# A four-stage graph network kernel: its last stage rewritten with full float32 matmuls, shared statistics and a later fourth norm

## The reference, cut to what matters

```python
x = _layernorm(x + _L0_gnn_ref(...))   # two graph convolutions and LSTMs
x = _layernorm(x + _L1_gnn_ref(...))   # masked attention
x = _layernorm(x + _L2_gnn_ref(...))   # aggregation, two layers with batch norm
x = _layernorm(x + _L3_gnn_ref(...))   # below, J = 128 here

adj_0, adj_1, adj_2 = diag(adj), triu(adj, 1), tril(adj, -1)
h = einsum('bjf,kfo->kbjo', x, W)      # W is [3, 128, 128]
out = sum over k of einsum('ij,bjo->bio', adj_k, h[k]) + bias
```

## Time and profile before

| | us |
|---|---|
| median of 3 runs (lowest, highest) | 1770.82 (1768.04, 1772.41) |
| the profiled execution | 1766.66 |
| its span, first to last instruction | 1764.9 |
| busy in the span: PE, DVE, ACT, POOL | 1515.1, 1347.8, 1071.9, 461.5 |
| mean granted TensorE clock | 0.951 of 2.4 GHz |

### The profile page before, as it was taken

How to read it: one execution, slowest core, us unless ns; L and a number is a source line. 1 busy time by engine, 2 the same in 40 slices (tenths; PEclk the granted TensorE clock), 3 DMA queues, 4 the chain that set the end, 5 groups by cost and what they waited for, 6 DMA issues and landing times. The chain is left out here.

```text
span 1764.9 us, 29113 instructions
## 1 busy us (share of the span) xinstructions
PE 1515.1 (86%) x9300; PEld 1252.2 (71%) x9300; DVE 1347.8 (76%) x3193; ACT 1071.9 (61%) x2018; POOL 461.5 (26%) x699
## 2 busy tenths in 40 slices
PE   3998999899899989966999999999995996777775
PEld 3888888788888888964767767777774554555554
DVE  3578777767776777776888888888884556888886
ACT  3675675566665756744666666666662664666665
POOL 2122212212211222123333333333332002334333
PEclk9999999999999999987999999999997997989888
DMA  2000000000000000000000000000000000111111
GB/s 91 1 1 25 13 1 13 25 1 13 13 13 12 1 25 13 1 14 1 19 19 12 18 18 12 18 18 12 18 18 24 0 0 24 60 59 63 56 59 48
DMA packets 19515, 37.58 MB, mean 21 GB/s; under 512 B 3312, under 2 KB 4848, under 8 KB 19312
## 3 DMA queue, kind: packets, MB, share of 16 engines
q1 hardware_dynamic: 18576, 34.49, 6.1%
q10 hardware_dynamic: 864, 2.11, 0.3%
HBM read 19.81 MB, written 16.78 MB: 21 GB/s over the span
## 5 line engine op out<-in xcount | busy, mean ns | idle before, releaser
L377 PE MATMUL banks<-early_rounded 128*128 128x128 f32 (+3 forms) x1424 | 457.3, 321 | 63.6 <-DVE early_rounded L968 31.3
L378 PE MATMUL banks<-early_rounded 128*128 128x128 f32 (+3 forms) x1424 | 452.8, 318 | 0.0
L379 PE MATMUL banks<-early_rounded 128*128 128x128 f32 (+3 forms) x1424 | 452.6, 318 | 0.0
L773 ACT ACTIVATE early_scratch<-banks,consts 128x256 f32<-128x256 f32 (+2 forms) x624 | 312.1, 566 | 129.5 <-PE banks L379 115.0
L377 PEld LDWEIGHTS banks<-early_rounded 128*128 128x128 f32 x1424 | 279.0, 196 | 88.8 <-issue 41.4
L378 PEld LDWEIGHTS banks<-early_rounded 128*128 128x128 f32 x1424 | 279.5, 196 | 14.3
L379 PEld LDWEIGHTS banks<-early_rounded 128*128 128x128 f32 x1424 | 279.0, 196 | 13.8
L644 POOL CAST early_rounded<-early_scratch 128x512 fp32r<-128x512 f32 (+2 forms) x160 | 94.0, 597 | 550.5 <-DVE early_scratch L963 550.5
L487 POOL TENSOR_TENSOR consts<-consts 128x4 f32<-128x4 f32 (+1 forms) x112 | 125.9, 1124 | 151.3 <-DVE consts L461 148.8
L377 PE MATMUL banks<-kept_rounded 128*128 128x128 f32 (+2 forms) x384 | 142.7, 372 | 21.9 <-DVE kept_rounded L1117 5.5
L727 ACT ACTIVATE attention_rounded<-banks 32x512 fp32r<-32x512 f32 (+1 forms) x160 | 94.5, 591 | 98.4 <-PE banks L1305 67.9
(11 more groups left out here) (168 smaller groups left out, 3213.6 us busy)
## 6 DMA issues: line engine op xcount, KB each, us to landing
early_scratch<-in_x_dram SPq DMA_DIRECT2D x16, 512.0 KB, 3.6
x_away<-attention_scratch SPq DMA_DIRECT2D x32, 256.0 KB, 2.0
late_scratch<-x_away SPq DMA_DIRECT2D x32, 256.0 KB, 2.7
out_dram<-late_scratch SPq DMA_DIRECT2D x32, 256.0 KB, 2.0
x_all<-in_WihT_dram ACTq DMA_DIRECT2D x1, 1024.0 KB, 5.5
x_all<-in_WhhT_dram ACTq DMA_DIRECT2D x1, 768.0 KB, 7.2
x_all<-in_Wqkv_dram ACTq DMA_DIRECT2D x1, 192.0 KB, 9.8
kept_scratch<-in_W_dram SPq DMA_DIRECT2D x1, 192.0 KB, 2.4
```

Source lines behind the costliest of these rows:

```text
L377: pe.matmul(out, wt[0], mv[0], start=start, stop=False)
L378: pe.matmul(out, wt[1], mv[0], start=False, stop=False)
L379: return pe.matmul(out, wt[0], mv[1], start=False, stop=stop)
L773: nc.scalar.activation(gate_f[lane][gate][:, 0:cols], bank(bank_set("lstm", n, unit), gate)[:, 0:cols], ACT.Tanh if gate == G else ACT.Sig ...
```

## The change

Everything lies in the last stage. The mixing is one full float32 matmul for each batch and the sums are three, with x3, the adjacency parts and the weights as they are; the high and low parts of all of these go, and with them ACT's and POOL's work on x3, DVE's subtraction of each mix, and the splitting of two late weights earlier in the program. DVE works in rounds (`late_round`): the fourth norm's add and sums for the group four behind, the third norm's add and sums for the newest, the third norm's application for the one behind it, and then one set of small operations over eight columns, four of each norm. POOL raises eight columns at once. ACT applies the fourth norm six groups behind the newest, first in its head. There are two buffers for y3, y4, the mixes and the shifts, and four for x3. The diff leaves out what the functions printed above show of the old code.

```diff
+    def late_groups(eng, order, do):
+        def head_of(head, at):
+            for what, part, late in order:
+                if not isinstance(head, int) or 0 <= head - late < GROUPS:
+                    do(what, part, head - late, (at - late) % 4)
+        warm = 8
+        for head in range(warm):
+            head_of(head, head)
+        with eng.Fori(warm // 4, GROUPS // 4) as i:
+            for at in range(4):
+                head_of(i * 4 + at, at)
+        for head in range(GROUPS, GROUPS + max(late for _, _, late in order)):
+            head_of(head, head)
...
-        splits2 = [("w1", w1_r), ("w3", w3_r), ("hatT", hatT_r), ("adjk", adjk_r)]
+        splits2 = [("w1", w1_r), ("hatT", hatT_r)]
...
-        r2 = Area(sb("late_rounded", 6 * GC, F32R))
-        mix_r = pair(r2, GB * 3 * P)
-        f3 = Area(sb("late_scratch", 14 * GC))
-        hid_f = [[f3.take(GC) for _ in range(2)] for _ in range(2)]
-        z_f = f3.take(GC)
-        y3 = f3.take(GC)
-        x3_f = [f3.take(GC) for _ in range(2)]
-        y4 = f3.take(GC)
-        oT_f = f3.take(GC)
+        f3 = Area(sb("late_scratch", 21 * GC))
+        mix_f = [f3.take(GB * 3 * P) for _ in range(2)]
+        z_f, oT_f = f3.take(GC), f3.take(GC)
+        y3 = [f3.take(GC) for _ in range(2)]
+        y4 = [f3.take(GC) for _ in range(2)]
+        x3_f = [f3.take(GC) for _ in range(4)]
+        hid_f = [[y3[u], y4[u]] for u in range(2)]
+        late_small = f3.take(2 * 12 * 2 * GB)
...
+                wait_if(sp, y3_made, g - 1)
...
-            for g in range(3):
+            for g in range(6):
                 fetch(g, g % 2)
-            with sp.Fori(0, GROUPS // 2 - 2) as i:
+            with sp.Fori(0, GROUPS // 2 - 3) as i:
                 for u in range(2):
-                    fetch(i * 2 + (u + 3), (u + 1) % 2)
+                    fetch(i * 2 + (u + 6), u)
                     put(i * 2 + u, u)
-            fetch(GROUPS - 1, 1)
-            for g in range(GROUPS - 4, GROUPS):
+            for g in range(GROUPS - 6, GROUPS):
...
+                pool.wait_ge(late_var, g + 1)
+                wait_if(pool, out_ready, g - 5)
+                wait_if(pool, x3_kept, min(g - 1, GROUPS) if isinstance(g, int) else g - 1)
+                _, _, _, mean, var, rstd = late_cols(place % 2)
+                lo = GB if isinstance(g, int) and g >= GROUPS else 0
+                hi = GB if isinstance(g, int) and g < 4 else 2 * GB
+                nc.gpsimd.tensor_tensor(rstd[:, lo:hi], var[:, lo:hi], minus_half[:, lo:hi], ALU.pow)\
+                  .then_inc(late_rstd, 1)
+                pool.wait_ge(late_rstd, g + 1)
+                if hi == GB:
+                    nc.gpsimd.memset(shift_cols[:, (place % 2) * GB:(place % 2) * GB + GB], 0.0).then_inc(shift4, 1)
+                else:
+                    nc.gpsimd.tensor_tensor(shift_cols[:, (place % 2) * GB:(place % 2) * GB + GB],
+                                            mean[:, GB:2 * GB], rstd[:, GB:2 * GB], ALU.mult).then_inc(shift4, 1)
+            for head in range(8):
+                do("rstds", 0, head, head % 4)
+            with pool.Fori(2, GROUPS // 4) as i:
+                for at in range(4):
+                    do("rstds", 0, i * 4 + at, at)
...
-                if what == "x3":
-                    act.wait_ge(x3_kept, g + 1)
-                    wait_if(act, mixed, (g - 1) * GB)
-                    copy(x3_r[place][0], x3_f[place]).then_inc(x3_hi, 1)
                 if what == "mixed":
                     act.wait_ge(mixed, g * GB + part + 1)
-                    wait_if(act, w3_sums, g)
+                    wait_if(act, w3_sums, g - 1)
                     at = part * 3 * P
-                    copy(mix_r[0][:, at:at + 3 * P], banks[:, 2 + part, 0:3 * P]).then_inc(mixed_hi, 1)
+                    copy(mix_f[place % 2][:, at:at + 3 * P], banks[:, 2 + part, 0:3 * P]).then_inc(mixes_kept, 1)
                 if what == "sums":
                     act.wait_ge(w3_sums, g + 1)
                     wait_if(act, o_turned, g)
                     nc.scalar.activation(oT_f, banks[:, 1, :], ACT.Identity, bias=out_bias).then_inc(w3_kept, 1)
                 if what == "norm":
-                    act.wait_ge(shift4, g + 1)
-                    wait_if(act, out_stored[place], (g - place) * 8)
-                    _, (_, _, _, _, _, rstd) = ln_cols(1, GB)
+                    act.wait_ge(shift4, g + 5)
+                    wait_if(act, out_stored[place % 2], (g - place % 2) * 8)
+                    _, _, _, _, _, rstd = late_cols(place % 2)
                     for b in range(GB):
-                        ins = nc.scalar.activation(o_f[place][:, b * P:(b + 1) * P], y4[:, b * P:(b + 1) * P],
-                                                   ACT.Identity, bias=shift_cols[:, b:b + 1], scale=rstd[:, b:b + 1])
+                        at = (place % 2) * GB + b
+                        ins = nc.scalar.activation(o_f[place % 2][:, b * P:(b + 1) * P],
+                                                   y4[place % 2][:, b * P:(b + 1) * P], ACT.Identity,
+                                                   bias=shift_cols[:, at:at + 1], scale=rstd[:, GB + b:GB + b + 1])
                     ins.then_inc(out_ready, 1)
-            groups(act, [("x3", 0, 2), ("sums", 0, 3), ("scaled", 0, 0), ("mixed", 0, 2), ("mixed", 1, 2), ("mixed", 2, 2), ("mixed", 3, 2), ("norm", 0, 3)], do, pairs=3)
+            late_groups(act, [("norm", 0, 6), ("sums", 0, 4), ("scaled", 0, 0), ("mixed", 0, 3), ("mixed", 1, 3), ("mixed", 2, 3),
+                              ("mixed", 3, 3)], do)
...
+            def statistics(k, third, fourth, place):
+                st, d, m2, mean, var, _ = late_cols(place % 2)
+                lo, hi = (0 if third else GB), (2 * GB if fourth else GB)
+                d, m2, mean, var = (col[:, lo:hi] for col in (d, m2, mean, var))
+                st = st[:, lo:hi, :]
+                dve.wait_ge(late_work, k * 3 + 1)
+                nc.vector.tensor_tensor(d, st[:, :, 1], st[:, :, 4], ALU.subtract)
+                nc.vector.scalar_tensor_tensor(out=m2, in0=st[:, :, 2], scalar=P * EPS, in1=st[:, :, 5],
+                                               op0=ALU.add, op1=ALU.add).then_inc(late_work, 1)
+                dve.wait_ge(late_work, k * 3 + 2)
+                nc.vector.scalar_tensor_tensor(out=var, in0=d, scalar=0.25, in1=d, op0=ALU.mult, op1=ALU.mult)
+                if third:
+                    nc.vector.scalar_tensor_tensor(out=mean[:, 0:GB], in0=d[:, 0:GB], scalar=0.5, in1=st[:, 0:GB, 4],
+                                                   op0=ALU.mult, op1=ALU.add)
+                if fourth:
+                    nc.vector.scalar_tensor_tensor(out=mean[:, -GB:], in0=d[:, -GB:], scalar=-0.5,
+                                                   in1=st[:, -GB:, 4], op0=ALU.mult, op1=ALU.subtract)
+                nc.vector.tensor_scalar(m2, m2, 1.0 / P, None, ALU.mult).then_inc(late_work, 1)
+                dve.wait_ge(late_work, k * 3 + 3)
+                nc.vector.tensor_tensor(var, m2, var, ALU.add).then_inc(late_var, 1)
+            def add_third(g, place):
+                st = late_cols(place % 2)[0]
+                dve.wait_ge(z_turned, g + 1)
+                wait_if(dve, late_rstd, g - 1)
+                wait_if(dve, x3_kept, g - 1)
+                dve.wait_ge(x2_loaded[place % 2], (g - place % 2) * 8 + 16)
+                nc.vector.tensor_tensor(y3[place % 2], banks[:, 0, :], x2_back[place % 2], ALU.add)\
+                  .then_inc(y3_made, 1)
+                dve.wait_ge(y3_made, g + 1)
+                for b in range(GB):
+                    ins = nc.vector.bn_stats(st[:, b, :], y3[place % 2][:, b * P:(b + 1) * P])
+                return ins
+            def add_fourth(g, place):
+                st = late_cols(place % 2)[0]
+                dve.wait_ge(o_turned, g + 1)
+                wait_if(dve, out_ready, g - 1)
+                nc.vector.tensor_tensor(y4[place % 2], banks[:, 6, :], x3_f[place], ALU.add).then_inc(y4_made, 1)
+                dve.wait_ge(y4_made, g + 1)
+                for b in range(GB):
+                    ins = nc.vector.bn_stats(st[:, GB + b, :], y4[place % 2][:, b * P:(b + 1) * P])
+                return ins
+            def norm_third(g, place):
+                _, _, _, mean, _, rstd = late_cols(place % 2)
+                dve.wait_ge(late_rstd, g + 1)
+                wait_if(dve, y4_made, g - 3)
+                wait_if(dve, mixed, (g - 3) * GB)
+                for b in range(GB):
+                    ins = nc.vector.tensor_scalar(x3_f[place][:, b * P:(b + 1) * P],
+                                                  y3[place % 2][:, b * P:(b + 1) * P], mean[:, b:b + 1],
+                                                  rstd[:, b:b + 1], ALU.subtract, ALU.mult)
+                ins.then_inc(x3_kept, 1)
+            def late_round(k, at):
+                third = not isinstance(k, int) or k < GROUPS
```

(32 more changed lines are left out.)

72 lines of the change are left out of this document (20 added, 52 removed).

## The result

The changed kernel takes **1686.56 us** (median of 4 runs, 1683.82 to 1689.47) against 1770.51 (1768.04 to 1772.41): a ratio of 0.9527, 95% interval 0.9502 to 0.9552, so 84 us less. The prediction said 1694, between 1684 and 1723. The profiled execution took 1689.47 us, its span is 1687.7.

A forecast was written before the change was run, and what follows sets the result against it. DVE's splitting of the mixes bounded the last stage at 8.73 us a round; afterwards the PE-ACT chain would, at 6.24. Start, 31 rounds (193.4 us) and 9.8 at the end saved 77 us: 1694 us, range 1684 to 1723.

The forecast's parts named there:

- PE's own round, 5.98: PE's work per last-stage round: sums 2.58, mixing 2.58, two transpose sets 0.82 us; 6.1 with a restart after a wait.
- The 2.9 us: Alternative price of PE's sums, twelve passes at 0.24 us instead of 2.58 us; forecast would be some 10 us later.
- The chain through ACT, 6.24: Last-stage loop of PE's sums, ACT's eviction, scaling and four copies, back to next sums: 6.24 us, the forecast round.
- the choice that four copies stand end to end: ACT's four copies of the mixes taken without overlap, 2.05 us; with overlap 1.7, chain 5.9, time 4 us less.
- the tenth for a restart: A tenth of a microsecond added to PE's 2.58 us sums for restarting after a wait.
- the lower bound of its range: PE's own round of 6.1 instead of 6.24 and splits uncovered, 1687; three more for run spread, 1684 us.
- POOL and the later norm: POOL's eight-column power takes 1.80 us; ACT's fourth norm stays hidden with 0.3 us to spare.
- The rival of the late norm: Late norm holds ACT's sums eviction; with two more microseconds, 6.9 us a round, 1713 us; 10% beyond the forecast's bounds.
- the two clock rivals: PE's clock stays at 0.90 or near, 1730 us (13%); or stays low throughout, 1874 us (3%).
- Start and end: First sums at 1482.1, 31 rounds of 6.24 to last sums at 1675.5, then 9.8 us: stage ends at 1685.3.
- The early part: Dropping two weight splits beside attention, costed at nothing; worth 3 us if uncovered.
- The signs named in advance: Right: adds 6.2 to 6.4 us apart, PE awaiting ACT's copies; wrong: adds 7 us apart, ACT's norm mostly awaiting POOL.

The follow-up runs named there:

- experiment 6: Changed kernel with the splitting into high and low parts put back for mixing and sums, keeping its order, lags, buffers and shared statistics: 1719.5 us, ratio 0.9723.
- experiment 2: Changed kernel with most of the mixing of two of the four batches left out (64 of 384 columns computed): 1676.5 us, one run.
- experiment 1: Changed kernel with ACT applying the fourth norm five groups behind the newest instead of six: 1811.5 us, one run.
- experiment 3: Changed kernel with shared statistics undone, small operations and POOL's power done over four columns twice: 1689.4 us, ratio 0.9536.
- experiments 7 and 11: Changed kernel with the two late weight splits put back: 1682.4 us; changed kernel unaltered, run again on another chip: 1684.0 us.
- experiment 4: Changed kernel with sums formed batch by batch, mixes stationary, no turn back or ACT eviction, POOL adding the bias to x3: 1672.5 us, ratio 0.9435.
- experiment 8: Sums-by-batch kernel with mixing as three rounded matmuls again, x3 split by ACT and POOL, bias added right behind: 1683.1 us, ratio 0.9525.
- experiment 9: Sums by batch with x3 split, but POOL adds the bias only after DVE's third norm of the next group: 1682.9 us, ratio 0.9498.

## Why the prediction was right, and where it was not

- **The bound.** Predicted: DVE no longer bounds, PE and ACT do. Shown: PE is busy in 60.00 of 60 us and DVE waits for it; experiment 6 gives the other side.
- **PE's own round, 5.98.** Measured 6.03: sums and mixing 2.57 and 2.58 as forecast from the earlier trace rows and three quarters of it, the two turns 0.44 each instead of 0.41. The 2.9 us that the prediction worked out from four passes of 0.24 us is refuted: the sums took 2.57, or 0.214 us for each of twelve passes, which is 514 cycles at 2.4 GHz for 512 columns. So the number of passes fits; the 0.24, taken from rounded matmuls, was not the price of one.
- **The chain through ACT, 6.24.** This is the mis-sized term. The step was the choice that four copies stand end to end, 2.05 us; they took 1.70 here and 1.62 in experiment 2, with 0.488 us for one: three overlaps of 0.08 to 0.11 us. The Trainium skill (ScalarE: Activation LUTs, What ACT_TABLE_LOAD costs) says that consecutive ACTIVATEs overlap by about 93 ns; these rows agree, and I had let outweigh it. Rows of the kernel before spoke for the overlap too: the four instructions of the fourth norm take 1.65 us where one lasts 0.48, and the scaling's overlap of 0.11 is in the prediction's own chain. Why the copies of the earlier trace rows don't overlap is open. Their output type is not the reason, since in experiment 6 copies of the mixes to fp32r, 0.487 us each, do overlap (64 of them in 25.8 us); what sets them apart in the rows is their 32 partitions. The other links hold, the tenth for a restart among them: the sums take 2.68 us behind a wait (experiment 2) and 2.57 without one. With the overlap the chain is 5.84 us, PE bounds, and 31 rounds are 0.21 x 31 = 6.5 us shorter than forecast. The prediction had this case as the lower bound of its range, and there the median lies.
- **POOL and the later norm.** Forecast 1.80 us for the power and 0.3 us to spare; measured 1.63 and, by ACT's wait for the sums behind the norm, 0.32. That the six groups keep the norm off the path is shown by experiment 1. The rival of the late norm would have had to find over 0.3 us; experiment 3 delayed it and cost 0.06 us a round.
- **The clock.** At 0.51 in the stage's first us before, 0.50 after, 0.95 up to 1540 us and 1.00 from there: the two clock rivals fall. PE had no gap there at all, where I had expected a small one in each head.
- **Start and end.** First sums 14.5 us into the stage by forecast; they start at 1488.35, 13.0 after 1475.31 (the first mixing comes 7.1 us into the stage, not 8.5). The stage came out at 209.7 us, forecast 1685.3 - 1467.6 = 217.7: 1.5 of the 8.0 are the start, 6.5 the rounds. The end, 9.8 us from the last sums at 1675.21, is as forecast.
- **The early part.** Costed at nothing. In the profiled execution it was 7.7 us longer, and so that execution's 1689.5 fell on the 1690 of the sum by two errors that cancel, which is luck. About 2.5 us of it recur with the splits' going (experiments 7 and 11), where the prediction allowed for nothing or a gain of 3. The median lies 7 us below the forecast, about as far as the stage is shorter than forecast; the early part's share in it is within the spread of the runs.
- **The signs named in advance.** ACT's norm does wait for POOL in nearly every head (28 times, 28.9 us), which the prediction had named as a sign of being wrong. It was a bad sign: ACT has that time to spare, and the norm still ends before the sums that ACT must serve. Two other signs, adds 6.2 to 6.4 us apart and PE waiting for ACT's copies, did not come, because the chain through ACT was priced too high.

## What to carry to other kernels

Where two bounds stand side by side, an engine's work and a ring of waits, price both halves of a rewrite and expect the sum of the halves to fall short of the whole: here 27 and 47 us each alone, and 85 both at once. In a list that an engine takes in order, a step that waits for another engine is placed by how many rounds its input needs, and one group too few cost 125 us here, more than the whole change gained. When PE has become the bound, look for a product whose operands can trade places so that its result comes out as the next step reads it.

## What the runs showed of the hardware

DVE can stand still for as long as a POOL instruction lasts. Beside POOL's addition of two tensors of 512 columns (1.27 to 1.29 us in experiment 4) DVE's third norm went from 0.338 to 0.625 us an instruction in the mean (experiment 8): one of its four took 1.28 to 1.46 us in each of 27 rounds, the other three at most 0.5. A DVE operation on eight columns with two SBUF inputs went from 0.168 to 1.261 us (experiment 9). Row sums, and adds that read PSUM, kept their time beside POOL's subtraction of x3's parts, which has two inputs of the same size. The Trainium skill (SBUF — State Buffer, Who interferes with whom) says that a DVE instruction in a mode with two ports, or with two SBUF inputs, and a POOL instruction that reads SBUF exclude each other for the whole instruction. Experiments 8 and 9 agree on DVE's side. POOL's addition took 1.28 to 1.40 us in experiment 8, so that POOL is held up for a whole instruction as well is not shown here. Room on POOL is therefore room only beside DVE's other work.
